# Token layers of a fused language model tower: attention scores from fp32 head slots instead of packed bf16 parts, with a new timetable

## What is computed

```
for i in range(N):                                   # N = 4
    q = (x @ Wq[i] + bq[i]) ; k = ... ; v = ...      # split in H = 8 heads of DK = 16
    scores = jnp.einsum('bhqd,bhkd->bhqk', q, k) * scale
    attn = jax.nn.softmax(scores, axis=-1)
    o = jnp.einsum('bhqk,bhkd->bhqd', attn, v)
    x = _layernorm(x + o @ Wo[i] + bo[i], g1[i], be1[i])
    f = jax.nn.relu(x @ W1[i] + b1[i]) @ W2[i] + b2[i]
    x = _layernorm(x + f, g2[i], be2[i])
```

## Time and profile before

| what | value |
|---|---|
| median of three runs | 1270.87 us |
| profiled execution, its time | 1284.4 us |
| profiled execution, its span | 1282.5 us |
| mean granted PE clock | 0.899 |
| PE / DVE / ACT / POOL busy | 1031.8 / 694.6 / 610.9 / 418.5 us |
| L2322, M matmuls (256 columns, bf16, 512 of them) | 99.8 us busy |
| L2343, S matmuls (256 columns, bf16, 512 of them) | 101.6 us busy |
| L2512, DVE maxima (256) | 167.5 us busy |
| L2457, ACT exponentials (256) | 149.9 us busy |

### The profile page before, as it was taken

How to read it: one execution, slowest core, us unless ns; L and a number is a source line. 1 busy time by engine, 2 the same in 40 slices (tenths; PEclk the granted TensorE clock), 3 DMA queues, 4 the chain that set the end, 5 groups by cost and what they waited for, 6 DMA issues and landing times. The chain is left out here.

```text
span 1282.5 us, 20645 instructions
## 1 busy us (share of the span) xinstructions
PE 1031.8 (80%) x7048; PEld 715.2 (56%) x7048; DVE 694.6 (54%) x1957; ACT 610.9 (48%) x1369; POOL 418.5 (33%) x460
## 2 busy tenths in 40 slices
PE   1368998999999998636797999977999999734787
PEld 1124555655556554323685677865887778622454
DVE  4266666777776675126353111151666666756663
ACT  3235565666666665326434533253444444330455
POOL 5313666566675674657003000134000000031110
PEclk9669999999999999867698899996999999955788
DMA  7343543433354430020000011100000100007440
GB/s 86 74 115 77 131 97 77 115 77 76 76 150 99 94 77 3 1 57 12 1 1 9 25 33 34 30 1 13 13 10 9 35 2 1 2 13 136 76 86 27
DMA packets 52391, 65.70 MB, mean 51 GB/s; under 512 B 9628, under 2 KB 45880, under 8 KB 49208
## 3 DMA queue, kind: packets, MB, share of 16 engines
q1 hardware_dynamic: 49256, 62.35, 21.7%
q0 software_dynamic: 512, 1.05, 1.3%
q10 hardware_dynamic: 2520, 0.99, 0.4%
HBM read 47.09 MB, written 17.27 MB: 50 GB/s over the span
## 5 line engine op out<-in xcount | busy, mean ns | idle before, releaser
L2512 DVE TENSOR_REDUCE t_nmax<-banks 128x2 f32<-128x512 f32 x256 | 167.5, 687 | 65.7 <-PE banks L2322 62.6
L2457 ACT ACTIVATE t_probs<-banks 128x512 f32<-128x512 f32 x256 | 149.9, 593 | 70.0 <-PE banks L2343 66.2
L2343 PE MATMUL banks<-t_packed 99*128 99x256 bf16 x512 | 101.6, 282 | 24.7 <-DMA t_packed<-t_max_parts 24.0
L2322 PE MATMUL banks<-t_packed 96*128 96x256 bf16 x512 | 99.8, 280 | 23.9 <-DMA t_packed<-t_qk_pairs 21.0
L1874 ACT ACTIVATE l_probs<-banks,l_shift 128x256 f32<-128x256 f32 x128 | 59.6, 470 | 118.3 <-DVE l_shift L1913 118.3
L2602 POOL TENSOR_SCALAR xhat<-t_rbuf,mv,rstd 128x128 f32<-128x128 f32 x128 | 100.5, 799 | 3.4
L2322 PEld LDWEIGHTS banks<-t_packed 96*128 96x128 bf16 x512 | 45.9, 99 | 85.5 <-issue 52.1
L2343 PEld LDWEIGHTS banks<-t_packed 99*128 99x128 bf16 x512 | 44.4, 100 | 77.3 <-issue 35.3
L2357 PE MATMUL banks<-t_probs,t_v 128*32 128x256 f32 x1024 | 85.3, 402 | 0.1
L707 POOL TENSOR_TENSOR n_rstd<-n_vareps,mhalf 128x4 f32<-128x4 f32 x4 | 4.0, 1008 | 237.6 <-DVE n_nmean L690 237.5
L1548 ACT ACTIVATE hid<-banks,b 128x512 f32<-128x512 f32 x64 | 43.5, 687 | 68.9 <-PE banks L1453 68.3
(11 more groups left out here) (364 smaller groups left out, 2321.3 us busy)
## 6 DMA issues: line engine op xcount, KB each, us to landing
t_qk_pairs<-t_parts SPq DMA_DIRECT2D x32, 384.0 KB, 2.6
t_packed<-t_qk_pairs SPq DMA_DIRECT2D x32, 384.0 KB, 6.2
t_packed<-t_qk_pairs SPq DMA_DIRECT2D x32, 256.0 KB, 6.3
g_packed<-g_qk_parts SPq DMA_DIRECT2D x48, 128.0 KB, 4.4
t_packed<-t_qk_pairs SPq DMA_DIRECT2D x32, 128.0 KB, 7.2
w<-in_L_ffn_w SPq DMA_DIRECT2D x16, 256.0 KB, 2.6
g_qk_parts<-g_parts SPq DMA_DIRECT2D x8, 384.0 KB, 5.5
wff<-in_L_tok_W SPq DMA_DIRECT2D x8, 256.0 KB
```

Source lines behind the costliest of these rows:

```text
L2322: ins = pe.matmul(m.mbank[:, n % 3, i * S:(i + 1) * S], m.packed[0:MROW, 0, p, h, c + qt * P:c + (qt + 1) * P], m.packed[0:MROW, 1, p, h, ...
L2343: ins = pe.matmul(m.sbank[:, n % 2, i * S:(i + 1) * S], m.packed[0:MROW + 3, 1, p, h, c + kt * P:c + (kt + 1) * P], m.packed[0:MROW + 3, 0 ...
L2457: act.activation(m.probs[:, n % 6, :], m.sbank[:, n % 2, :], ACT.Exp).then_inc(sem["probs_ready"], 1)
L2512: dve.tensor_reduce(m.nmax[:, b, u // 4, 2 * hp:2 * hp + 2], m.mbank[:, n % 3, :].rearrange("p (i k) -> p i k", i=2), AX.X, ALU.max, negat ...
```

## The change

- **q and k stay fp32 in slots.** Each head has a slot of 32 partitions: 16 dimensions, one row for the maximum, the rest zero. Four heads fill 128 partitions, so q and k take two halves each: the projections become four (`Aq0`, `Aq1`, `Ak0`, `Ak1`, 128x512 fp32), each emptied by one ACT instruction. The splitting, both trips through DRAM and the packed tiles are gone from the token layers.
- **M and S steps** are now one head each, two fp32 matmuls of 256 columns with a contraction of 32 rows, both in the row quarter u % 4 of PE. The steps are still 16 and 16.
- **The maxima** are written by DVE into row 16 of each slot, turned in fp32 (`MT00` to `MT11`, four steps instead of two) and added to q by DVE (`ad00` to `ad11`), in place of eight small DVE operations, two ACT copies and the DRAM trip. k has a one in that row through its bias.
- **AV** is four steps instead of eight, each with twice the matmuls. `probs` has eight buffers instead of six.
- **The timetable** is new: `PERIOD` is 23.66 instead of 25.065 and all numbers of `PLACES` differ.
- **Wide attention:** projections lie two to a unit over six units instead of three over four, and ACT has an order of its own: the copy of T and the next head's WT step come ahead of the exponentials.
- The set-up before the first layer prepares the slots and the bias with the ones row instead of constants of the packed tiles.

The core of the diff:

```diff
-PERIOD = 25.065
+PERIOD = 23.66
 PLACES = {
     "pe": (
-        ("Aq", 190.54), ("Ak", 192.28), ("V", 194.32), ("M0.0", 213.04), ("M0.1", 213.8), ("M0.2", 214.45), ("M0.3",
+        ("Aq0", 0.0), ("Aq1", 4.47), ("Ak0", 11.39), ("Ak1", 14.9), ("M0.0", 15.44), ("M0.1", 17.85), ("M0.2", 19.23),
...
                     b, u = int(step[1]), int(step[3])
-                    n, qt, c = 16 * g + 8 * b + u, u // 4, b * S
-                    if b == 0 and u == 0:
-                        pe.wait_ge(sem["packed"][p], 16 * 6 * (l + 1))
+                    n, half, rows, c = 16 * g + 8 * b + u, u // 4, head_rows(u), b * S
+                    if b == 0 and u % 4 == 0:
+                        pe.wait_ge(sem["q_ready"], 4 * g + 3 + half)
                     if n >= 3:
                         pe.wait_ge(sem["max_taken"], n - 2)
-                    for i in range(2):
-                        h = 2 * (u % 4) + i
-                        ins = pe.matmul(m.mbank[:, n % 3, i * S:(i + 1) * S],
-                                        m.packed[0:MROW, 0, p, h, c + qt * P:c + (qt + 1) * P],
-                                        m.packed[0:MROW, 1, p, h, c:c + S], start=True, stop=True)
+                    for qt in range(2):
+                        ins = pe.matmul(m.mbank[:, n % 3, qt * S:(qt + 1) * S], m.q[rows, p, half, c + qt * P:c + (qt + 1) * P],
+                                        m.k[rows, p, half, c:c + S], start=True, stop=True)
...
-                    if u == 0:
-                        pe.wait_ge(sem["mrow"][b], 16 * (g + 1))
+                    if u % 4 == 0:
+                        pe.wait_ge(sem["max_added"], 4 * g + 2 * b + half + 1)
                     if n >= 2:
                         pe.wait_ge(sem["probs_ready"], n - 1)
-                    for i in range(2):
-                        h = 4 * hq + 2 * hp + i
-                        ins = pe.matmul(m.sbank[:, n % 2, i * S:(i + 1) * S],
-                                        m.packed[0:MROW + 3, 1, p, h, c + kt * P:c + (kt + 1) * P],
-                                        m.packed[0:MROW + 3, 0, p, h, c:c + S], start=True, stop=True)
+                    for kt in range(2):
+                        ins = pe.matmul(m.sbank[:, n % 2, kt * S:(kt + 1) * S], m.k[rows, p, half, c + kt * P:c + (kt + 1) * P],
+                                        m.q[rows, p, half, c:c + S], start=True, stop=True)
...
-                    for i in range(4):
-                        ins = pe.matmul(m.obank[SLOT * i:SLOT * (i + 1), hq * S:(hq + 1) * S],
...
+                    for kt in range(2):
+                        for i in range(4):
+                            ins = pe.matmul(m.obank[SLOT * i:SLOT * (i + 1), half * S:(half + 1) * S],
...
+                elif step[0:2] == "ad":
+                    b, half = int(step[2]), int(step[3])
+                    key = ("MT%d%d" % (b, half), g)
+                    lin_ready(dve, *key)
+                    q = m.q[:, p, half, b * S:(b + 1) * S]
+                    dve.tensor_tensor(q, lin[turn[key][0]][:, 0:S], q, ALU.add).then_inc(sem["max_added"], 1)
...
+        scores = ("SC", n) if n < len(units) else None
+        turns = ("T", n - 2) if 2 <= n < len(units) + 2 else None
+        values = ("AV", n - 3) if n >= 3 else None
+        order += [x for x in (scores, turns, between[0], values, between[1]) if x]
+        act_order += [x for x in (turns, between[0], scores, values, between[1]) if x]
...
+    def head_rows(u):
+
+        return slice(SLOT * (u % 4), SLOT * (u % 4 + 1))
```

More of the change, by code:

```diff
@@ L1673, in wide_order @@
     units = [(h, b) for h in range(WH) for b in range(B)]
-    order = weights_of(0) + projections_of(0)
+    order = [("WT", 0), ("VO", 0)] + projections_of(0)
+    act_order = list(order)
     for n in range(len(units) + 3):
         h, b = divmod(n, B)
-        between = [None, None, None]
+        between = [None, None]
         if h + 1 < WH:
-            if b == 0:
-                between[0] = ("WT", h + 1)
-            elif b == 1:
-                between[1] = ("VO", h + 1)
-            elif 3 <= b < 7:
-                between = projections_of(h + 1)[3 * (b - 3):3 * (b - 2)]
-        steps = [("SC", n) if n < len(units) else None, ("T", n - 2) if 2 <= n < len(units) + 2 else None,
-                 ("AV", n - 3) if n >= 3 else None]
-        for step, item in zip(steps, between):
-            order += [x for x in (step, item) if x]
-    return units, order
+            if b < 2:
+                between[0] = ("WT", "VO")[b], h + 1
+            else:
+                between = projections_of(h + 1)[2 * (b - 2):2 * (b - 1)]
+        scores = ("SC", n) if n < len(units) else None
[3 more added lines that the diff above has]
+        act_order += [x for x in (turns, between[0], scores, values, between[1]) if x]
+    return units, order, act_order
 def wide_attention(nc, m, t, sem, settle, banks, stack, last_loads):
@@ L1834, in _ @@
         def _(act):
-            for item in order:
+            for item in act_order:
                 if item[0] == "WT":
@@ L2275, in _ @@
                             sp.wait_ge(sem[name], 16 * layer * len(loads))
-                elif step in ("sq", "sk"):
-                    store(0 if step == "sq" else 1, g)
-                elif step in ("lq", "lk"):
-                    load(0 if step == "lq" else 1, g)
-            for g in range(PAIRS):
-                sp.wait_ge(sem["packed"][g], 16 * 6 * LAYERS)
-            for b in range(2):
-                sp.wait_ge(sem["mrow"][b], 16 * LAYER_PAIRS)
         @block.tensor
@@ L2309, in _ @@
                     else:
-                        ins = pe.matmul(bank, w.qk(l, 0 if step == "Aq" else 1), m.xT[:, p * PW:(p + 1) * PW],
+                        ins = pe.matmul(bank, w.qk(l, int(step[1] == "k"), int(step[2])), m.xT[:, p * PW:(p + 1) * PW],
                                         start=True, stop=True)
@@ L2452, in _ @@
+                if step[0] == "f":
+                    k, half = int(step[1] == "k"), int(step[2])
+                    lin_ready(act, "A" + step[1:], g)
+                    act.activation((m.k if k else m.q)[:, p, half, :], lin[turn[("A" + step[1:], g)][0]], ACT.Identity,
+                                   bias=w.qk_bias(l, k, half), scale=1.0 if k else DK ** -0.5).then_inc(sem["q_ready"], 1)
                 elif step[0] == "E":
@@ L2726, in _ @@
             pe.wait_ge(sem["w_ordered"], 1)
-            pe.matmul(m.obank[:, 0:2 * LAYERS], ident_qk[:, :], qk_cols[:, :, :].rearrange("p l n -> p (l n)"),
-                      start=True, stop=True).then_inc(sem["lin_ready"][1], 1)
+            for half in range(2):
+                pe.matmul(m.obank[:, half * 2 * LAYERS:(half + 1) * 2 * LAYERS], into_slots[:, half, :],
+                          qk_cols[:, :, :].rearrange("p l n -> p (l n)"), start=True, stop=True)
+            pe.matmul(m.obank[:, 4 * LAYERS:4 * LAYERS + 1], into_ones[:, :], ones[:, :], start=True, stop=True
+                      ).then_inc(sem["lin_ready"][1], 1)
             for g in range(PAIRS):
```

223 lines of the change are left out of this document (76 added, 147 removed), and 39 rows, old and new, of the table PLACES.

## The result

The changed kernel takes 1751.0 us (median of 4 runs, 1743.18 to 1763.41). The kernel before took 1272.06 us on the same chip (4 runs, 1270.6 to 1281.38). The ratio is 1.3753 [1.3646, 1.386]. The direction was forecast, the size was not: 1751 lies 266 us above the forecast of 1485, and above its range.

The account below looks back on a forecast made before the run. PE was taken as the bound, at 45.6 us a pass instead of 28.45: layers +218, wide attention -4, so 1284.4 + 214 = 1498, less 13.5 for the median, forecast 1485 us; forecast range 1440 to 1530, 8-in-10 range 1415 to 1555.

Parts of the forecast that it names:

- What bounds the kernel: Token layers before the change: PE is the bound, busy 384.8 of 426.7 us; no other engine comes near.
- The work on PE: Token-layer pass after the change: all steps and waits together 45.6 us, against 28.45 before.
- the wait for t_oT: Token layers: C1, directly behind the second T2, waits for its copy, 0.5 us a pass.
- Quarters run side by side: M and S steps in different row quarters proceed independently, 23 times 0.86, 19.8 us a pass before entries.
- the rival of strict order: M and S steps start strictly in program order on PE: +3.9 us a pass, 1543 in all, chance 0.15.
- Entries cost nothing: Rival: entering and leaving quarters on PE is free: -4.8 us a pass, 1413 in all, chance 0.07.
- The clock: Token layers: PE runs at its upper level, 2.4 GHz, as the granted clock stood at 9 tenths or more.
- The sum: From first projection to last C4: 83 + 593 + 34 + 28 = 738 us, +218 against 520 before.
- The wide attention: PE's waits there for copies, 8.5 and 6.8 us, go in part: -4 us, between 0 and -15.
- the clock falls: Rival, token layers: lower level a sixth of the time, +7.6 us a pass, 1600 in all, chance 0.08.

Follow-up runs that it names:

- half rows: The changed kernel with M and S steps contracting 64 rows instead of 32, scores summed over two heads: 1569.5 us, ratio 1.2313 to before.

## Why the prediction was wrong

- **What bounds the kernel: right.** PE is busy 99% of the layers, DVE, ACT and POOL between 21% and 28%. No wait for a transfer is left.
- **The work on PE: right.** One pass at the upper level would be 64.9 x 0.71 = 46.1 us (an estimate), by 45.6 forecast. A lone step costs 1.06 (1.10 forecast), a projection 1.06 (0.93), AV 1.00 (1.10), MT 0.36 (0.25), the wait for t_oT 0.5 (0.5). These errors have both signs, so that the sum comes out closer than its terms.
- **Quarters run side by side: right.** The timeline of the changed kernel where M1.0 stands ahead of S1.5:

```profile
386.81 0.48 PE L2299 MATMUL banks<-t_k,t_q 32*128 32x256 f32 x1
386.83 0.48 PE L2317 MATMUL banks<-t_q,t_k 32*128 32x256 f32 x1
387.13 0.37 PE L2299 MATMUL banks<-t_k,t_q 32*128 32x256 f32 x1
387.15 0.37 PE L2317 MATMUL banks<-t_q,t_k 32*128 32x256 f32 x1
387.35 0.37 PE L2299 MATMUL banks<-t_k,t_q 32*128 32x256 f32 x1
...
387.88 1.07 PE L2330 MATMUL banks<-t_probs,t_v 128*32 128x256 f32 x16
```

  An fp32 matmul stands as two records, so the earlier step's first matmul is at 386.81 and 387.13 and its second begins at 387.35. The later step starts 0.02 us after the earlier one, and 0.52 ahead of the earlier step's second matmul. The two take 387.88 - 386.81 = 1.07, as one alone does. This ends the rival of strict order. The Trainium skill ("TensorE: Matmul & The Clock Gate", part 3, "The mechanism") has matmuls start and end strictly in program order; the trace disagrees for row quarters as it did for column quarters.
- **Entries cost nothing: wrong, as forecast.** The price was taken a little low: 0.24 a run, where half rows show 0.32, 0.20 of it in a lone step (1.06 where its four passes make 0.86) and the rest mostly in the whole-array step ahead of it. The Trainium skill ("TensorEngine Tiling (Array Packing)", "Key Properties") says that a change of the tiling mode drains the engine; the traces agree, with these 0.3 us.
- **The clock: the step that failed.** "The granted clock stands at 9 tenths or more" was read from a kernel whose steps on PE in the token layers all use at least 96 rows, and was carried to one where over half of the time goes to steps of 32. The mechanism stood among the rivals ("a row quarter leaves three quarters of the array idle"), at 0.08 and with a sixth of the time at the lower level. In fact it was 60% of the time (a mean of 0.70 between levels of 1.00 and 0.50). Against it the forecast put that PE hardly waits and that AV uses quarters too. Both are true and neither counts: PE was busy throughout the slow 36.3 us, and AV's quarters are column quarters with all 128 rows. The Trainium skill ("TensorE: Matmul & The Clock Gate", part 1, "What's actually happening") ties the level to how busy PE has been. The rows disagree if "busy" means that an instruction is running: PE was that for 787.2 of 792.9 us, at 0.70.
- **The sum.** First C4 84.8 us after the first projection (forecast 83); then 13 passes 853 (593); then 43 (34) and 29.5 (28); together 1010 against 738, +272. The clock's share can be read off: 0.30 of 792.9 us is 238 in the first 12 passes alone.
- **The wide attention: mis-sized.** SC's stretch went from 223.3 to 195.5 us, -28 where -4 was taken, between bounds of 0 and -15. The upper bound was the sum of two recorded waits. It left out a third wait, of 2.06 us, and the fall of the clock behind it, some 3.4, and the recorded waits are less than what they cost (0.44 against 0.57, 0.22 against 0.39). Layers and wide attention together: the last C4 comes 1010 us after the first projection instead of 520, +490, and -28 makes +462; the profiled executions differ by 1743.2 - 1284.4 = 459.

So "the clock falls" is the case that came, far larger than it was priced. Its price was also worked out wrongly: the forecast has the lower level for a sixth of the time and adds a sixth, 7.6 us, but half speed in a sixth of the time adds an eleventh, 4.1; a sixth is added where a sixth of the work runs slowly. Here it was 0.30 / 0.70 = 43% of the work, which makes 66.1 us of 46.3.

## What to carry to other kernels

In this kernel small fp32 matmuls in row quarters came near the price of the packed ones only where four steps, in four different quarters, stood one behind the other; alone, each costs nearly as much as the whole run of four (1.06 and 1.10 to 1.22 us), and where most of them stood alone the clock fell too. So before PE's order is laid out, take the price of each step from a trace, as a run and not as a share of a filled array, and place the runs first. And in a forecast, look at how much of the array the new steps use before the granted clock of the old kernel is carried over. Last, the recorded waits in front of an engine were less here than what their removal gave, and one of them had a fall of the clock behind it.

## What was not expected of the hardware

- PE can be busy without a gap and run at the lower level: 36.30 of 36.30 us busy, clock 0.50.
- The same order of the same number of matmuls shows, in the token layers, a clock of 1.00 with 128 rows or 64, 0.70 with quarters in turn, 0.65 with a single quarter; in an order that fills four quarters, 1.00 again. bf16 operands, with a lone step of 0.31 us instead of 1.06, give 0.99. Why the hardware does so, and where between these cases it begins, stays open.
- Rows that are not used can cost more than the steps that run side by side in them give: 1516.9 us with all rows and no step beside another, 1751.0 with quarters.
- Two fp32 steps in different quarters start 0.02 us apart and last 1.07 us, as one does; four last 1.22.
- Removing 15.0 us of recorded idle time of PE gave 27.7 us: some 3.4 of it is a fall of the clock behind a wait of 2.06 us, and part of the rest is idle time that is not recorded.
